# A routed-expert kernel in which one of the two scatter tables becomes the output itself

## What is computed

```python
x = x + tanh(g_ffn[1]) * L1_ffn(layernorm(x), ...)

# L1_ffn: 64 experts, every token goes to K = 4 of them, at most CAP = 128 tokens an expert
pos = (cumsum(oh, axis=0) * oh).sum(-1) - 1
valid = pos < CAP
xb = zeros((E, CAP, D)).at[eid, pos].set(flat[tok], mode='drop')
h = silu(einsum('ecd,edh->ech', xb, Wg)) * einsum('ecd,edh->ech', xb, Wu)
yb = einsum('ech,ehd->ecd', h, Wd)
y = yb[eid, minimum(pos, CAP - 1)] * (w * valid)[:, None]
out = zeros((N, D)).at[tok].add(y)
# and two shared experts that see every token
hs = silu(einsum('nd,sdh->nsh', flat, Sg)) * einsum('nd,sdh->nsh', flat, Su)
out = out + einsum('nsh,shd->nd', hs, Sd)
```

## Time and profile before

| | |
|---|---|
| median of 3 runs | 1206.94 us |
| the profiled execution | 1205.79 us, of which the span of the profile is 1203.8 us |
| PE busy | 1067.6 us, 89% |
| DVE, ACT, POOL busy | 673.7, 493.5, 555.4 us |
| DMA | 202.36 MB, 168 GB/s on average |
| the expert stage | from 919.57 us (first transposition) to 1160.33 us (end of the last addition's issue) |
| `finish` | from 1166.81 us (first load) to 1203.8 us |

### The profile page before, as it was taken

How to read it: one execution, slowest core, us unless ns; L and a number is a source line. 1 busy time by engine, 2 the same in 40 slices (tenths; PEclk the granted TensorE clock), 3 DMA queues, 4 the chain that set the end, 5 groups by cost and what they waited for, 6 DMA issues and landing times. The chain is left out here.

```text
span 1203.8 us, 18795 instructions
## 1 busy us (share of the span) xinstructions
PE 1067.6 (89%) x5503; PEld 756.9 (63%) x5503; DVE 673.7 (56%) x1558; ACT 493.5 (41%) x874; POOL 555.4 (46%) x523
## 2 busy tenths in 40 slices
PE   4999999999958999999788799999998999999920
PEld 2565555555356777777278568577676777788720
DVE  4577777776336888887476526456222333343426
ACT  2566565665316888887433031221311222222200
POOL 3344544644333666666334646457150334443530
PEclk9999999999967999999898999999999999999965
DMA  9954466643444333332540221032016999999639
GB/s 305 307 175 133 169 215 212 214 159 120 155 160 149 105 105 105 105 109 83 172 140 1 99 70 49 27 91 71 27 47 239 358 352 322 285 311 354 184 77 363
DMA packets 115964, 202.36 MB, mean 168 GB/s; under 512 B 19847, under 2 KB 28039, under 8 KB 115898
## 3 DMA queue, kind: packets, MB, share of 16 engines
q1 hardware_dynamic: 95802, 167.47, 40.7%
q0 software_dynamic: 20096, 34.08, 10.2%
HBM read 133.36 MB, written 87.03 MB: 183 GB/s over the span
## 5 line engine op out<-in xcount | busy, mean ns | idle before, releaser
L1929 POOL DMA_INDIRECT sums<-summary,m_token x64 | 99.2, 1550 | 161.3 <-DMA sums<-summary,m_token 89.6
L943 POOL TENSOR_TENSOR m_down_lo<-wo,m_down_hi 128x512 fp32r<-128x512 f32 x80 | 133.2, 1685 | 80.7 <-ACT m_down_hi L1018 80.7
L461 PE MATMUL bank<-win,vT 128*128 128x512 f32 x256 | 124.1, 597 | 0.0
L631 DVE TENSOR_REDUCE negmax<-bank 128x1 bf16<-128x512 f32 x128 | 86.9, 679 | 48.3 <-PE bank L468 48.0
L554 ACT ACTIVATE win<-bank 128x512 f32<-128x512 f32 x128 | 69.5, 595 | 105.5 <-PE bank L453 105.4
L1032 DVE TENSOR_TENSOR m_up_lo<-w,m_up_hi 128x1024 fp32r<-128x1024 f32 x80 | 98.9, 1238 | 10.2 <-ACT m_up_hi L1005 8.4
L1952 PE MATMUL bank<-y,m_w 128*128 128x128 f32 x736 | 89.7, 275 | 0.0
L1242 POOL DMA_INDIRECT tab<-stage_up,slot x64 | 65.2, 1018 | 50.3 <-DVE slot L1577 32.0
L468 PE MATMUL bank<-k_hi,q_parts 128*128 128x512 f32 x128 | 76.2, 595 | 12.7 <-DVE negmax L631 9.2
L1952 PEld LDWEIGHTS bank<-y,m_w 128*128 128x128 f32 x736 | 86.4, 193 | 0.5 <-issue 0.5
L2107 PE MATMUL bank<-w_sd,stage_gate 128*128 128x512 f32 x192 | 85.8, 603 | 0.3 <-DVE stage_gate L2097 0.3
(11 more groups left out here) (285 smaller groups left out, 2430.1 us busy)
## 6 DMA issues: line engine op xcount, KB each, us to landing
tab<-zeros SPq DMA_DIRECT2D x16, 1056.0 KB, 11.8
m_w<-in_L_ffn_Wg SPq DMA_DIRECT2D x46, 256.0 KB
m_w<-in_L_ffn_Wu SPq DMA_DIRECT2D x46, 256.0 KB
m_w<-in_L_ffn_Wd SPq DMA_DIRECT2D x46, 256.0 KB
m_x<-tab SPq DMA_DIRECT2D x40, 256.0 KB, 2.7
ytab<-m_y SPq DMA_DIRECT2D x40, 256.0 KB, 2.0
stage_up<-tab SPq DMA_DIRECT2D x32, 264.0 KB
m_x<-tab SPq DMA_DIRECT2D x32, 264.0 KB
```

Source lines behind the costliest of these rows:

```text
L461: nc.tensor.matmul(pO[s * 2 + h][:], vT[:, s, sb_, h:h + 2, :].rearrange("p a c -> p (a c)"), probs[:, sb_ % 2, h, :], start=(sb_ == 0), s ...
L631: nc.vector.tensor_reduce(negmax[:, s, m:m + 1], pM[:], AX.X, ALU.max, negate=True).then_inc(pm_read, 1)
L943: nc.gpsimd.tensor_tensor(dn_lo[:, m, :], row(wo0, e * MB + m), dn_hi[:, m, :], ALU.subtract).then_inc(dn_lo_ready, 1)
L1929: nc.gpsimd.indirect_dma_start(T["sums1"][e % SUMS], bass.IndirectOffsetOnAxis(token[:, e % META:e % META + 1], 0), y[:, e % RING, :], Non ...
```

## The change

- `out`, seen as 2048 rows, takes the place of the second table (`tables = T["sums1"], T["out_rows"]`). Only one table is left to be filled with zeros.
- Before routed rows are added to it, `out` must hold x plus the shared experts' part. So SP stores `x_sb` to `out` at the end of `middle`'s programs: groups 0, 1 and 2 in one DMA each, group 3 in four, each when its tiles have had the shared part added. POOL waits for all seven (`out_begun`) before its first addition.
- For that the down projection of group 3 is made in `middle`, after its gate and up projections, and the part of `experts` that did it is gone.
- W_EARLY becomes 11: the weights of experts 3 to 10 are all issued in `middle`, ahead of group 3's four stores.
- `finish` is now four DMAs on POOL's queue, with addition, from `sums1` to `out`, DRAM to DRAM, 1 MB each; nothing is loaded to SBUF, and DVE and SP have no part in it.

```diff
-W_EARLY = 6
+W_EARLY = W_RING - 1
...
-        sums1 = [nc.dram_tensor(f"sums1_{n}", (B * SEQ, D), F32, kind="Internal").ap() for n in range(SUMS)]
+        sums1 = nc.dram_tensor("sums1", (B * SEQ, D), F32, kind="Internal").ap()
+        out_rows = out.rearrange("b t d -> (b t) d")
...
@@ middle, tensor
-                    if with_down(g):
-                        shared.down(pe, g, j, pY, chunk(g, SharedExperts.CHUNKS - 1, 1) + 1)
-                        if prepared(g):
-                            for run, k in between[j]:
-                                run(g + 1, k)
-                if with_down(g):
+                    shared.down(pe, g, j, pY, chunk(g, SharedExperts.CHUNKS - 1, 1) + 1)
+                    if prepared(g):
+                        for run, k in between[j]:
+                            run(g + 1, k)
+                if prepared(g):
 
                     need(pe, shared.y_read, g * TPB + TPB)
...
@@ middle, vector
-                    if with_down(g):
-                        shared.add(dve, g, j, g * TPB + j, pY)
+                    shared.add(dve, g, j, g * TPB + j, pY)
...
@@ middle, sync
+            def store(tiles, after):
+
+                sp.wait_ge(shared.y_read, after)
+                sp.dma_start(T["out_rows"].rearrange("(t p) d -> p t d", p=P)[:, tiles, :],
+                             x_sb[:, tiles, :]).then_inc(T["out_begun"], 16)
+
+            for g in range(2):
+                store(slice(g * TPB, g * TPB + TPB), g * TPB + TPB)
             sp.wait_ge(x2_ready, TILES - TPB)
             for e in range(2):
                 load_expert(sp, A, T, e, e)
             sp.wait_ge(lg_full, TILES)
             sp.wait_ge(fT_kept, TILES)
             load_expert(sp, A, T, 2, 2)
+            store(slice(2 * TPB, 3 * TPB), 3 * TPB)
...
             for e in range(3, W_EARLY):
                 load_expert(sp, A, T, e, e)
+            for t in range(3 * TPB, TILES):
+                store(slice(t, t + 1), t + 1)
...
@@ experts, gpsimd
+            pool.wait_ge(T["out_begun"], 16 * (B - 1 + TPB))
             for e in range(E1):
...
                 nc.gpsimd.indirect_dma_start(
-                    T["sums1"][e % SUMS], bass.IndirectOffsetOnAxis(token[:, e % META:e % META + 1], 0), y[:, e % RING, :], None,
+                    tables[e % SUMS], bass.IndirectOffsetOnAxis(token[:, e % META:e % META + 1], 0), y[:, e % RING, :], None,
...
@@ finish
+        PARTS = 4
+        sums, rows = (t.rearrange("(n p r) d -> n p (r d)", n=PARTS, p=P) for t in (T["sums1"], T["out_rows"]))
         block = c.enter_context(nc.Block())
...
+        @block.gpsimd
+        def _(pool):
+            for n in range(PARTS):
+                nc.gpsimd.dma_start(rows[n], sums[n], max_dma_last_dim=2 * 4 * D, accum_op=ALU.add).then_inc(stored, 16)
+            pool.wait_ge(stored, 16 * PARTS)
```

More of the change, by code:

```diff
@@ L117, in build @@
             s_w0 = arena0.enter_context(nc.semaphore("weights0_loaded"))
+            out_begun = ctx.enter_context(nc.semaphore("out_begun"))
             s_padded = ctx.enter_context(nc.semaphore("table0_padded"))
@@ L163, in build @@
                 experts(nc, A, T)
-            finish(nc, A, T, out)
+            finish(nc, T)
 def attention(nc, A, T):
@@ L277, in _ @@
             t1 = T["tab1"].rearrange("(n r p) d -> n p r d", p=P, n=ZERO_CHUNKS)
-            sums = [t.rearrange("(n r p) d -> n p r d", p=P, n=E0) for t in T["sums1"]]
+            sums = T["sums1"].rearrange("(n r p) d -> n p r d", p=P, n=E0)
             w01_v = w01[:].rearrange("p (e b) m -> p e b m", e=E0)
@@ L297, in behind @@
                         [P, E1 * CAP1 // (ZERO_CHUNKS * P), XW])).then_inc(s_zero1, 16)
[L298 to L301, removed]
+                chunk = sums[u] if isinstance(u, int) else sums[bass.ds(u, 1)].rearrange("o p r d -> p (o r) d")
+                sp.dma_start(chunk, zeros[:, 0:D].unsqueeze(1).broadcast_to(
+                    [P, B * SEQ // (E0 * P), D])).then_inc(s_zero1, 16)
             behind(0)
@@ L927, in step @@
                                  y[:, (q - 1) % 2, :]).then_inc(stored[(q - 1) % 2], 16)
-            sp.wait_ge(T["s_zero1"], 16 * (ZERO_CHUNKS + SUMS * E0 + 1))
+            sp.wait_ge(T["s_zero1"], 16 * (ZERO_CHUNKS + E0 + 1))
             sp.wait_ge(T["s_padded"], 16 * E0)
@@ L1147, in middle @@
         SPLITS = [(w, s) for w in (1, 0) for s in range(NSH)]
-        groups_done = B - 1
         NORMED = ((4, 7), (0, 7))
@@ L1206, in with_shared @@
             return 0 <= g
-        def with_down(g):
-            return 0 <= g < groups_done
         @block.gpsimd
@@ L1222, in inverse_std @@
                 nc.gpsimd.tensor_tensor(rstd[:, a:z_], ve[:, a:z_], power[:, a:z_], ALU.pow).then_inc(rstd_ready, 1)
-            pool.wait_ge(T["s_zero1"], 16 * (ZERO_CHUNKS + SUMS * E0 + 1))
+            pool.wait_ge(T["s_zero1"], 16 * (ZERO_CHUNKS + E0 + 1))
             def gather(n, tiles):
@@ L1873, in experts @@
         bank, ident = T["bank"], T["ident"]
-        x_sb, hidden, w_sd = T["x_sb"], T["hidden"], T["w_sd"]
         RING = 4
@@ L1895, in experts @@
         y_full, y_ready = sem("m1_y_full"), sem("m1_y_ready")
[L1896 to L1899, removed]
+        pX, pH, pY = bank[0:2], bank[2:4], bank[4:6]
+        tables = T["sums1"], T["out_rows"]
         block = c.enter_context(nc.Block())
-        def back_at(i):
-            return divmod(i - BACK, CHUNKS) if 0 <= i - BACK < TPB * CHUNKS else None
         @block.sync
@@ L1954, in _ @@
                     last.then_inc(h_full, 1)
[L1955 to L1963, removed]
                 if valid(i - 1, n=E1):
@@ L2004, in _, with finish @@
                                             ALU.mult).then_inc(y_ready, 1)
[L2005 to L2013, removed]
+def finish(nc, T):
@@ L2015, in finish @@
     c = ExitStack()
     with c:
[L2017 to L2028, removed]
@@ L2029, in finish @@
-        sums = [t.rearrange("(t p) d -> p t d", p=P) for t in T["sums1"]]
-        block = c.enter_context(nc.Block())
[L2032 to L2053, removed]
+        stored = c.enter_context(nc.semaphore("out_stored"))
+        PARTS = 4
```

## The result

The changed kernel takes 1213.38 us (median of six runs, 1209.07 to 1217.08), against 1206.12 for the kernel before (six runs, 1202.85 to 1207.4). The ratio is 1.006, with a 95% interval of 1.0037 to 1.0083: slower by 0.6%, with an interval that reaches down to 0.4%. The forecast was 1216, with the largest chance on slower by more than 0.5%.

What follows compares the result with a forecast made beforehand. PE was taken to set the expert stage's pace with DMA hardly behind, and DMA to bound `finish`. 1203.8 + 16 (stage) - 5.5 (`finish`) = 1214.3 of span, with 2.0 around it 1216; range 1201 to 1232.

Steps and rivals of the forecast that it cites:

- 1. The move: Shared down projection moved to `middle`: takes 27.8 us, expert stage begins 25 us later, of PE alone a gain of 4.
- 2. What the transfers do: Expert stage: lost load time (+12) and additions holding PE, steps settling between 3.5 and 4.08 us: +16 us.
- My upper bound of +25: Expert stage: five additions at 3.12 us and 43 at 4.08 reach expert 48 at 1142, against 1117.20.
- rival C: Expert stage: PE keeps 3.12 us throughout (-4), additions not slowed by a short backlog; 1197 in all, chance 0.08.
- 3. Additions to `out`, the seven stores: Expert stage: additions to `out` and POOL's wait for seven stores cost 0, bounds 0 and +3 us.
- 4. `finish`: `finish`: DRAM to DRAM addition at 155 GB/s takes 27 us, 31.5 in all: -5.5 us, bounds -10.5 and +1.3.
- rival B: Stage loses bare bandwidth only (+9 to +12), addition in `finish` runs at 185 to 189 GB/s (-10.5): no difference; chance 0.27.
- the 26 to 39 us: Sign for `finish`: the prediction is wrong if its duration falls outside this range.
- My worse end: `finish`: DRAM traffic, two reads and a write per byte, limited to 363 GB/s; 12.6 MB take 35 us: +2.
- rival D: `finish`: addition takes 40 us or more, +8 or more, with +16 in the stage: 1231; from 115 GB/s down; chance 0.15.
- The rule of the Trainium skill: `finish`: about 2.0 us plus bytes over 436e3 per us, so 9.6 us for the bytes and 1200 in all.
- 5. Fewer zeros: Attention: 4 MB fewer writes of zeros change the time by 0, bounds -2 and 0 us.

Runs made afterwards that it cites:

- `three_tables`: The changed kernel with three tables in turn (two of sums and `out`), not two; first to last addition 208.7 us, against 225.9 in the changed kernel.
- `eight_buffers`: The changed kernel with eight result buffers in place of four; first to last addition 224.2 us, against 225.9 in the changed kernel.
- `move_only`: The kernel before with only group 3's down projection made in `middle` and 11 experts' weights issued there; ratio 1.0161 to before, 1226.89 us.
- `cover_kept`: The kernel before with `out` as a table and the new `finish`, the 32 shared matmuls left in the experts' steps; ratio 0.9934 to before, 1200.04 us.
- `fewer_bytes`: The changed kernel with loads of Wu and Wd of experts 12 to 63 cut to a quarter; first to last addition 205.1 us, against 225.9.
- `one_block`: `cover_kept` with its five final additions put at the end of POOL's program in `experts`; ratio 0.9931 to the kernel before.

## Why the prediction was right

**1. The move.** I had the stage begin 25 us later and the shared work take 27.8; it began 24.2 us later by U, and took 27.63. Right. A detail that I had not reckoned with: before, PE sat idle for 4.82 us ahead of the stage, and its granted clock from 920 to 925 us was 0.69 of 2.4 GHz, a mean of its two levels (1.2 and 2.4 GHz), and the first transpositions took 1.95 us; now PE comes from work at the upper level (1.00), and they take 1.20. The first addition is therefore only 23.1 us later.

**2. What the transfers do.** +16 was forecast, and +19.4 measured to the last addition, +20.1 to the start of `finish`. The sum stood, but its split was wrong. I gave +12 to the bytes and 4 to the additions' hold on PE. `three_tables` shows 6.1 for the bytes and 14.1 for the additions. The wrong step was to treat the additions as a pace that comes and goes with the backlog, and "settles between 3.5 and 4.08": they go at 3.89 us from the second on until the loads end. Their chain has nearly one length in every kernel with two tables and full loads, 224.2 to 231.2 us, whether PE has shared matmuls in its steps or not. Before, the steps of 3.98 us hid it: the shared matmuls filled a time in which PE would have had to wait. Taken out, they shorten the chain by 3.7 us (229.6 to 225.9), and put its start later by 23.1 us from U (14.4 to 37.5). My upper bound of +25 was worked out from this very chain, at 4.08 us; I gave it too little weight.

The length alone would not have told this ahead, though: before, the mean from expert 1 to 48 is 3.93 us, but part of these intervals are PE's own steps. From 1042 to 1072 us every addition waits for DVE's result, at 3.98 and then at 3.12 us:

```profile
1054.38 1.55 POOL L1929 DMA_INDIRECT sums<-summary,m_token  x1 [2.43 <-DVE summary L2003]
1071.99 1.55 POOL L1929 DMA_INDIRECT sums<-summary,m_token  x1 [1.57 <-DVE summary L2003]
```

That PE's step with a shared matmul (3.98) is just what the chain asks for (3.89) is a coincidence of this kernel. No run relaxes the chain with the shared matmuls left in place.

I had also written that 3.12 us would last for the first few experts and that past the tenth I would be wrong (rival C). It lasted for 14, since the four buffers take up 0.8 us of lag an expert for longer than I had reckoned; `eight_buffers` doubles this to 32 without any gain at the end. The sign that I named was a poor one: PE's steps don't show whether the additions lag, POOL's do. C itself, PE at 3.12 us over the whole stage, did not happen.

**3. Additions to `out`, the seven stores.** Cost 0, as forecast: the first addition waits for DVE (52.51 us idle, released by `summary`), not for the stores, and `move_only` has the loss without either.

**4. `finish`.** -5.5 was forecast, -13.1 measured. The mechanism is right, the rate was mis-sized: 155 GB/s, where it is 212. I had taken a value between the mean of one short addition (133) and its best slices (189). The long stream runs above the best slices: its 4 KB packets take 328 ns (4.2 MB in about 20 us). That is rival B's half, and more than B gave it (-10.5). It also puts `finish` outside the 26 to 39 us that I had named as a sign of being wrong: the pace of the step was mis-sized. The experiments say what did not make it quick: not the 4 KB pieces (206 GB/s with 2 KB) and not the source. What is left is the length of the stream, which I put into one sentence and then halved; that the start of each short addition is what slows it is argued from the earlier trace rows, not shown by a run. My worse end, DRAM traffic as a bound at 363 GB/s, is refuted: counted as I counted it there, as two reads and a write, 212 GB/s would be 636, and a source in SBUF was no quicker. (The 636 is worked out; no trace shows the read of the destination.) Nor was 363 the highest rate of the trace for plain transfers: in `finish` before they ran at 380 GB/s from 1170 to 1200 us. And with the 4.5 us that I put around the step, `finish` would have been no shorter than before from 129 GB/s down, not from 115 as rival D has it. The rule of the Trainium skill (DMA: Bandwidth & Descriptors, Anatomy of one DMA), by which `finish` would take some 14 us (an estimate: 9.6 for the bytes, and the 4.5 around them), does not hold for additions here either: it took 23.9.

**5. Fewer zeros.** The last up projections ended 3.5 us earlier in the profile of after. Over the twelve kernels U lies between 910.22 and 916.20 without a pattern (`move_only`, with both tables, has the latest, but `three_tables`, with both, 914.29, is earlier than `cover_kept`, with one), so I read it as spread and not as a gain; whether a fraction of a us is in it stays open.

The errors of 2 and 4, +4 and -7.6, partly cancelled, and the profiled run was a quick one; so the median of 1213.4 came near the forecast of 1216 with less merit than the figures suggest. The direction was right, and so was that the shared matmuls were a cover; but the larger part of what they covered was the waits for landings and not the loads' bytes, and that the total fits is in part luck. Both signs of being wrong that I had named showed (14 steps at 3.12 us, `finish` at 23.9), and the last weights were issued 17.4 us later (20.9 from U) where I had 12 to 16.

## What to carry to other kernels

Before moving work out of a stage in which PE is 100% busy, look for the slowest chain that runs through it, here additions that must land one after the other on two tables: take the interval at which its links go where they wait for each other and not for PE, here 4.08 us in the trace of before, and hold it against PE's step without the work, 3.12. If it is longer, PE's work up to the difference is nearly free in the stage, and moved out it costs: here 19.4 us for 27.6. (The mean interval of the whole stage will not do, since where PE is slower it is PE's step.) To find out what holds such a stage, lengthen the buffers and relax the chain in separate runs: the buffers moved PE's end by 12 us and the end of the stage by 2, the third table moved both. A change that joins a good part and a bad one should be taken apart: the new `finish` with the old order is 0.7% faster than before, where the whole was 0.6% slower.

## What the runs showed of the hardware that I had not expected

- A DMA with addition, in a long stream, runs at 204 to 212 GB/s, from DRAM or from SBUF, in pieces of 2 or of 4 KB. The last routed addition, 0.26 MB with nothing beside it, has 124 to 133.
- The landing of an addition is slower under load even where its own bytes are few: 3.9 us an expert with the DMA share at 1.0, 3.4 in `fewer_bytes` (from expert 1 to 48), with shares of 0.84 to 0.99, and 2.7 with the loads over. By the packets of the traces part of it passes before the data moves: the first data packet of the last addition before (1158.78) starts 2.1 us after the issue, and those at full load, where they can be told apart, 3 to 5 us after it.
- 5.5 us pass between the issue of a routed addition and the issue of what waits for it on POOL, with nothing but additions in flight (1156.82 to 1162.28 in `one_block`).
